# ScalarE's and VectorE's order, and the value product's place, in an attention and group-norm kernel

## The chip, the cores and the metric

One core of a Trainium2 chip runs the kernel. The time is device microseconds of one execution; the median of several executions is compared. The engines have one queue each and run their instructions in the order written: TensorE (PE in the profile, its weight loads PEld), VectorE (DVE), ScalarE (ACT), GpSimd (POOL) and SyncE (SP), which only starts transfers here. They wait for each other through semaphores.

## What is computed

```python
# x: (32, 128, 1024), y = ctx_4096: (32, 128, 1024), weights 128x128, 8 heads
q = Wq @ y + bq;  k = Wk @ y + bk;  v = Wv @ x + bv          # per batch, (heads, 16, 1024)
scores = einsum('bhdl,bhel->bhde', q, k) / sqrt(128)         # over channels: 16x16 per head
out = einsum('bhde,bhel->bhdl', softmax(scores), v)
o = Wo @ out + bo + x
result = (o - mean(o)) * rsqrt(var(o) + 1e-5) * gn_w + gn_b  # mean and variance over a whole batch item
```

## The kernel before

The scores need only y's Gram matrix G = y y^T (128x128) and y's row sums. So each of the 32 batch items becomes a short chain: Gram matrix, query product, scores, softmax, two small products that fold Wo, the softmax and Wv into one 128x128 matrix m (the identity is added for the residual), one wide product o = m x, and a normalisation whose statistics come from o's mean and variance by bn_stats. What is called a batch below is one such item.

For the Gram matrix, y comes transposed, as [128, 8 chunks, 128]. ScalarE rounds it to fp32r (`round_half`, L325), VectorE writes the rest y - rounded beside it (`rest_half`, L456), and TensorE multiplies in 8 passes, one for each chunk, with 258 columns (`gram`, L672). A pass gives rounded by rounded and rounded by rest; the second part is copied by ScalarE (`copy_cross`, L339), transposed back by TensorE (`transpose_cross`, L689) and added (`add_gram`, L475). Sums of the rest go through GpSimd (`fold_first` to `fold_last`, L243 to L284) into the same PSUM tile.

Then, for batch b: `query` (L711) and `add_query_bias` (L495); `scores` (L722) with `scale_bk` (L341); `minimum` (L506); `exponential` (L351), `invert_sum` (L517) and `normalise` (L361) make the softmax a_sb; `softmax_product` (L730) gives r in PSUM, `copy_r` (L367) copies it to r_sb, and `value_product` (L739) multiplies it by Wv. `fold_matrix` (L523) writes m_sb, the sum's waits included; `pivot_column` (L533) makes a column from which the mean is shifted. `input_product` (L746) computes o in two halves of 512 columns, each read by `statistics_of` (L542). `aggregate`, `deviation` and `square` (L548 to L566) go into `statistics` (L758), a product with ones that sums over partitions; `negative_variance`, `variance` (L568 to L600), GpSimd's power (`inverse_deviation`, L286) and ScalarE's `write_gain`, `write_shift` (L375 to L389) make scale and offset, and `output` (L391) writes the 1024 columns of the result, in one operation per batch, which SyncE stores.

All of this is software-pipelined by hand. Every engine has its own loop over t from 4 to 36 (`range(4, B + LAGS)`), and in turn t it works on up to five batches: input product and statistics of t-4, softmax and value products of t-3, query and scores of t-2, Gram matrix of t-1, rounding of t, output of t-5. The order within a turn is the order of the calls. In the last five turns (t = 32 to 36) the calls for batches that don't exist return at once, so these turns are the same order with holes. TensorE's turn is: two input halves, softmax product, query, four Gram passes, value product, four Gram passes, scores, statistics, transposition. The value product waits for r_copied. o_ps has room for two batches, so input_product(b) waits until the output of batch b-2 has been written (normed); the last batch has its two halves in g_ps and ps_ps.

## Time and profile before

| | us |
|---|---|
| median of 3 runs | 168.95 (168.01 to 169.55) |
| the profiled execution | 167.54 |
| its span, first to last instruction | 165.6 |
| mean granted clock of TensorE | 0.992 of full speed |
| median time to landing of a load of y (512 KB) | 6.1 |

The profile is of one execution, and all durations below are from it; its own time lies 1.4 us under the median. Rows of a timeline give the start, the duration, engine, line of the kernel and operation, with what is written and read; a row may stand for several instructions (x2, x4) that follow each other. Rows of a pipelined engine overlap: the next may start a tenth of a microsecond before the end of the one before, so the distance of starts, not the duration, is what an operation costs its engine. Brackets give idle time ahead of a row and what ended it. All of TensorE's products are recorded at one line, L666, and are told apart by their tiles. An fp32 product takes two weight loads and two matmuls.

### The profile page before, as it was taken

How to read it: one execution, taken by the hardware profiler on the slowest of the kernel's cores; microseconds unless marked ns; L12 is line 12 of the kernel's file. 1: busy time of each engine (PE TensorE's matmuls, PEld its weight loads, DVE VectorE, ACT ScalarE, POOL GpSimd, SP SyncE). 2: the span in 40 equal slices, each digit the busy share in tenths (PEclk: the TensorE clock that was granted, in tenths of full speed). 3: DMA queues.
4: the chain of work that ended last, by engine and by line, in shares of the span. 5: the costliest groups of instructions: out<-in, count | busy, mean ns of one | idle time of the engine just before them, and what ended most of it. 6: DMA issues, size and time to landing. Idle time of an engine off the chain costs nothing. (4 is left out here: it accounts for less than half of the span.)

```text
span 165.6 us, 3745 instructions
## 1 busy us (share of the span) xinstructions
PE 155.0 (94%) x932; PEld 121.8 (74%) x932; DVE 150.7 (91%) x686; ACT 138.9 (84%) x354; POOL 98.3 (59%) x162
## 2 busy tenths in 40 slices
PE   7998999999999999999999999999999999999720
PEld 7896888777777788877777778888777777886400
DVE  1788999999999999999999999999999999987661
ACT  3784599999999999999999989999999999977441
POOL 3049366777666676667766667666776666651110
PEclk9999999999999999999999999999999999999996
DMA  5999769999999999999999999999999987732333
GB/s 187 410 417 410 291 223 287 334 330 333 354 381 298 303 350 364 352 345 346 344 351 313 366 340 340 340 336 334 334 356 377 364 311 262 251 130 101 124 145 139
DMA packets 14276, 50.82 MB, mean 307 GB/s; under 512 B 1712, under 2 KB 1712, under 8 KB 14256
## 3 DMA queue, kind: packets, MB, share of 16 engines
q1 hardware_dynamic: 13824, 50.08, 83.4%
q10 hardware_dynamic: 432, 0.53, 0.9%
q8 instruction: 7, 0.11, 0.3%
q14 instruction: 13, 0.11, 0.2%
HBM read 33.82 MB, written 16.78 MB: 305 GB/s over the span
## 5 line engine op out<-in xcount | busy, mean ns | idle before, releaser
L666 PE MATMUL o_ps<-x_sb,m_sb 128*128 128x512 f32 x124 | 60.8, 613 | 0.0
L666 PE MATMUL g_ps<-hl_sb 128*128 128x258 f32 x256 | 46.4, 304 | 0.0
L456 DVE TENSOR_TENSOR hl_sb<-y_sb,hl_sb 128x512 fp32r<-128x512 f32 x64 | 44.0, 692 | 0.0
L325 ACT CAST hl_sb<-y_sb 128x512 fp32r<-128x512 f32 x64 | 40.0, 629 | 2.1 <-DMA y_sb<-in_ctx_dram 2.0
L546 DVE BATCH_NORM_STATS2 bn<-o_ps 128x6 f32<-128x512 f32 x62 | 40.3, 687 | 1.6 <-PE o_ps L666 1.6
L404 ACT ACTIVATE out_sb<-o_ps,shift,gain 128x1024 f32<-128x1024 f32 x31 | 37.5, 1210 | 0.1
L252 POOL TENSOR_TENSOR lsuma<-hl_sb 128x256 f32<-128x256 f32 x30 | 21.9, 731 | 25.3 <-DVE hl_sb L456 25.3
L666 PEld LDWEIGHTS g_ps<-hl_sb 128*128 128x128 f32 x256 | 35.0, 191 | 0.2 <-DVE hl_sb L456 0.2
L263 POOL TENSOR_TENSOR lsumb<-hl_sb 128x256 f32<-128x256 f32 x30 | 21.9, 729 | 18.1 <-DVE hl_sb L456 18.1
L666 PEld LDWEIGHTS o_ps<-x_sb,m_sb 128*128 128x128 f32 x124 | 21.2, 191 | 14.8 <-issue 14.8
L274 POOL TENSOR_TENSOR lsum<-lsuma,lsumb 128x256 f32<-128x256 f32 x30 | 22.4, 747 | 4.2 <-issue 0.4
L293 POOL TENSOR_TENSOR rstd<-veps,nhalf 128x1 f32<-128x1 f32 x32 | 17.6, 550 | 11.9 <-DVE veps L599 11.9
L666 PEld LDWEIGHTS rm_ps<-w_in,a_sb 128*128 128x128 f32 x64 | 12.0, 189 | 14.9 <-ACT a_sb L365 7.8
L365 ACT ACTIVATE a_sb<-a_sb,zinv 128x128 f32<-128x128 f32 x32 | 12.9, 402 | 7.5 <-DVE zinv L521 7.5
L358 ACT ACTIVATE a_sb<-sc_sb,smin 128x128 f32<-128x128 f32 x32 | 12.9, 402 | 3.4 <-DVE smin L513 3.3
L284 POOL TENSOR_TENSOR lsum<-lsum 128x128 fp32r<-128x128 f32 x30 | 14.3, 476 | 2.4
L666 PE MATMUL st_ps<-st_in,onesn 128*128 128x3 f32 (+2 forms) x66 | 10.5, 229 | 3.0 <-DVE st_in L538 1.5
L666 PE MATMUL rm_ps<-r_sb,w_in 128*128 128x128 f32 x64 | 12.6, 278 | 0.5 <-ACT r_sb L373 0.4
L666 PEld LDWEIGHTS st_ps<-st_in,onesn 128*128 128x128 f32 x66 | 9.8, 188 | 4.3 <-DVE st_in L564 3.8
L666 PE MATMUL ps_ps<-w_in,p_sb 128*128 128x128 f32 x64 | 12.5, 277 | 0.0
L666 PE MATMUL ps_ps<-wqT,g_sb 128*128 128x128 f32 x64 | 12.5, 277 | 0.0
L349 ACT ACTIVATE sbk_sb<-bkB,s_sb 128x128 f32<-128x128 f32 x32 | 12.3, 386 | 0.1
(76 smaller groups left out, 287.8 us busy)
## 6 DMA issues: line engine op xcount, KB each, us to landing
y_sb<-in_ctx_dram SPq DMA_DIRECT2D x32, 512.0 KB, 6.1
x_sb<-in_x_dram SPq DMA_DIRECT2D x32, 512.0 KB, 6.9
out_dram<-out_sb SPq DMA_DIRECT2D x31, 512.0 KB, 6.0
w_in<-in_weights_dram ACTq DMA_DIRECT2D x1, 256.0 KB, 5.6
out_dram<-out_sb ACTq DMA_DIRECT2D x1, 256.0 KB, 2.6
out_dram<-out_sb SPq DMA_DIRECT2D x1, 256.0 KB, 2.8
cols<-in_columns_dram ACTq DMA_DIRECT2D x1, 3.0 KB, 3.5
```

The costliest lines, as they stand in the source:

```text
L252: nc.gpsimd.tensor_tensor(lsuma[:, :, :], part[:, 0:HCH // 2, :], part[:, HCH // 2:HCH, :], ALU.add).then_inc(lsuma_ready, 1)
L263: nc.gpsimd.tensor_tensor(lsumb[:, :, :], part[:, 0:HCH // 2, :], part[:, HCH // 2:HCH, :], ALU.add).then_inc(lsumb_ready, 1)
L274: nc.gpsimd.tensor_tensor(lsum2[:, :, :], lsuma[:, :, :], lsumb[:, :, :], ALU.add).then_inc(lsum2_ready, 1)
L284: nc.gpsimd.tensor_tensor(lsum[:, b % 2, :], lsum2[:, 0, :], lsum2[:, 1, :], ALU.add).then_inc(lsum_ready, 1)
L293: nc.gpsimd.tensor_tensor(rstd[:, b % 2:b % 2 + 1], veps[:, b % 2:b % 2 + 1], nhalf[:, :], ALU.pow).then_inc(rstd_ready, 1)
L325: nc.scalar.copy(hl_sb[:, b % SLOTS, chunks, 0:C], y_sb[:, b % SLOTS, chunks, :]).then_inc(h_ready, 1)
L358: nc.scalar.activation(a_sb[:, b % 2, :], sc_sb[:, b % 2, :], ACT.Exp, bias=smin[:, b % 2:b % 2 + 1], scale=-1.0, accum_out=zsum[:, b % 2: ...
L365: nc.scalar.mul(a_sb[:, b % 2, :], a_sb[:, b % 2, :], zinv[:, b % 2:b % 2 + 1]).then_inc(a_ready, 1)
L404: nc.scalar.activation(out_sb[:, b % SLOTS, :], o_ps[:, b % 2, :], ACT.Identity, bias=shift[:, b % 2:b % 2 + 1], scale=gain[:, b % 2:b % 2 ...
L456: nc.vector.tensor_tensor(hl_sb[:, b % SLOTS, chunks, C:2 * C], y_sb[:, b % SLOTS, chunks, :], hl_sb[:, b % SLOTS, chunks, 0:C].bitcast(F3 ...
L546: nc.vector.bn_stats(bn[:, b % 2, half, :], o_half(b, half)).then_inc(bn_done, 1)
L666: return nc.tensor.matmul(dst, lhsT, rhs, start=start, stop=stop, **more)
```

## The change

Five things change. In ScalarE's loop, the first rounding of a batch moves to the end of the turn before, the second in between the exponential and the normalisation, and `copy_r` stands ahead of `write_shift`, so that the output follows the shift. In VectorE's loop, `invert_sum` moves behind the next turn's `copy_sum`, and `fold_matrix` and `pivot_column` go ahead of `deviation` and `square`. In TensorE's loop, the value product stands behind two Gram passes, not four. The loops end at t = 31, and each of the three engines has an order of its own written out for what the last five turns did. There, the input product of the last three batches waits for m_sb and x directly, and the variance of the last four waits for an earlier rstd. GpSimd's and SyncE's loops stay as they are.

```diff
--- before.py
+++ after.py
@@ -421,18 +421,46 @@
             scale_bk(1)
             copy_r(0)
             copy_cross(2)
-
-            for t in range(4, B + LAGS):
+            round_half(4, 0)
+
+            for t in range(4, B):
                 exponential(t - 3)
+                round_half(t, 1)
                 normalise(t - 3)
                 write_gain(t - 5)
                 scale_bk(t - 2)
+                copy_r(t - 3)
                 write_shift(t - 5)
-                copy_r(t - 3)
-                round_half(t, 0)
                 output(t - 5)
                 copy_cross(t - 1)
-                round_half(t, 1)
+                round_half(t + 1, 0)
+
+            b = LAST
+            exponential(b - 2)
+            normalise(b - 2)
+            scale_bk(b - 1)
+            write_gain(b - 4)
+            write_shift(b - 4)
+            copy_r(b - 2)
+            output(b - 4)
+            exponential(b - 1)
+            copy_cross(b)
+            normalise(b - 1)
+            scale_bk(b)
+            copy_r(b - 1)
+            write_gain(b - 3)
+            write_shift(b - 3)
+            output(b - 3)
+            exponential(b)
+            normalise(b)
+            copy_r(b)
+            write_gain(b - 2)
+            write_shift(b - 2)
+            output(b - 2)
+            write_gain(b - 1)
+            write_shift(b - 1)
+            output(b - 1)
+            output(b)
 
         @block.vector
         def _(dve):
@@ -595,6 +623,9 @@
             def variance(b):
                 if not live(b):
                     return
+                if b >= LAST - 3:
+
+                    dve.wait_ge(rstd_ready, b - 1)
                 dve.wait_ge(nvar_ready, b + 1)
                 nc.vector.tensor_scalar(veps[:, b % 2:b % 2 + 1], nvar[:, b % 2:b % 2 + 1], -1.0, EPS,
                                         ALU.mult, ALU.add).then_inc(veps_ready, 1)
@@ -638,18 +669,19 @@
             add_gram(2)
             invert_sum(1)
 
-            for t in range(4, B + LAGS):
+            for t in range(4, B):
                 copy_sum(t - 2)
                 if t > 4:
+                    invert_sum(t - 3)
                     rest_half(t - 1, 1)
                 statistics_of(t - 4, 0)
                 statistics_of(t - 4, 1)
                 add_query_bias(t - 2)
                 aggregate(t - 4)
+                fold_matrix(t - 3)
                 deviation(t - 4)
-                fold_matrix(t - 3)
+                pivot_column(t - 3)
                 square(t - 4)
-                pivot_column(t - 3)
                 rest_half(t, 0)
                 minimum(t - 2)
                 negative_variance(t - 4)
@@ -657,7 +689,60 @@
                 weighted_shift(t - 4)
                 variance(t - 4)
                 add_gram(t - 1)
-                invert_sum(t - 2)
+
+            b = LAST
+            copy_sum(b - 1)
+            invert_sum(b - 2)
+            statistics_of(b - 3, 0)
+            rest_half(b, 1)
+            add_query_bias(b - 1)
+            statistics_of(b - 3, 1)
+            aggregate(b - 3)
+            fold_matrix(b - 2)
+            minimum(b - 1)
+            deviation(b - 3)
+            pivot_column(b - 2)
+            square(b - 3)
+            invert_sum(b - 1)
+            negative_variance(b - 3)
+            variance(b - 3)
+            add_gram(b)
+            copy_sum(b)
+            weighted_shift(b - 3)
+            statistics_of(b - 2, 0)
+            add_query_bias(b)
+            fold_matrix(b - 1)
+            statistics_of(b - 2, 1)
+            minimum(b)
+            shift_by_pivot(b - 2)
+            pivot_column(b - 1)
+            invert_sum(b)
+            aggregate(b - 2)
+            statistics_of(b - 1, 0)
+            deviation(b - 2)
+            square(b - 2)
+            statistics_of(b - 1, 1)
+            negative_variance(b - 2)
+            variance(b - 2)
+            fold_matrix(b)
+            shift_by_pivot(b - 1)
+            aggregate(b - 1)
+            pivot_column(b)
+            deviation(b - 1)
+            weighted_shift(b - 2)
+            square(b - 1)
+            statistics_of(b, 0)
+            negative_variance(b - 1)
+            shift_by_pivot(b)
+            weighted_shift(b - 1)
+            variance(b - 1)
+            statistics_of(b, 1)
+            aggregate(b)
+            deviation(b)
+            square(b)
+            negative_variance(b)
+            variance(b)
+            weighted_shift(b)
             last_output()
 
         @block.tensor
@@ -669,21 +754,22 @@
                 for _ in range(count):
                     product(o_ps[:, 1, 0:P], onesn[:, :], onesn[:, :])
 
-            def gram(b, half):
-                if not live(b):
-                    return
-                pe.wait_ge(l_ready, 2 * b + 1 + half)
-                if half == 0 and b >= 1:
+            def gram(b, chunks):
+                if not live(b):
+                    return
+
+                pe.wait_ge(l_ready, 2 * b + (1 if chunks[-1] < HCH else 2))
+                if chunks[0] == 0 and b >= 1:
 
                     pe.wait_ge(g_copied, b)
                     if b <= EARLY:
                         pe.wait_ge(high_copied, b)
                     else:
                         pe.wait_ge(s_copied, b)
-                for c in range(half * HCH, (half + 1) * HCH):
+                for c in chunks:
                     mm = product(g_ps[:, 0:HL], hl_sb[:, b % SLOTS, c, 0:C], hl_sb[:, b % SLOTS, c, :],
                                  start=(c == 0), stop=(c == CH - 1))
-                if half == 1:
+                if chunks[-1] == CH - 1:
                     mm.then_inc(hl_ready, 1)
 
             def transpose_cross(b):
@@ -747,9 +833,10 @@
                 if not live(b):
                     return
                 if half == 0:
-
-                    if b == LAST:
-                        pe.wait_ge(pivot_ready, b + 1)
+                    if b >= LAST - 2:
+                        pe.wait_ge(m_copied, b + 1)
+                        pe.wait_ge(x_in[b % SLOTS], loads(b))
+
                     if 2 <= b < LAST:
 
                         pe.wait_ge(normed, b - 1)
@@ -772,38 +859,66 @@
             product(row_ps[:, :, :].rearrange("p v e -> p (v e)"), onesn[:, :],
                     diag[:, :, :].rearrange("p v e -> p (v e)")).then_inc(rows_ready, 1)
 
-            gram(0, 0)
-            gram(0, 1)
+            gram(0, range(0, HCH))
+            gram(0, range(HCH, CH))
             low_sum(0, range(0, HCH))
             transpose_cross(0)
             low_sum(0, range(HCH, CH))
             keep_busy(FILL)
             query(0)
-            gram(1, 0)
-            gram(1, 1)
+            gram(1, range(0, HCH))
+            gram(1, range(HCH, CH))
             scores(0)
             transpose_cross(1)
             low_sum(1, range(0, CH))
             query(1)
-            gram(2, 0)
+            gram(2, range(0, HCH))
             softmax_product(0)
-            gram(2, 1)
+            gram(2, range(HCH, CH))
             value_product(0)
             scores(1)
             transpose_cross(2)
             statistics(-1)
 
-            for t in range(4, B + LAGS):
+            for t in range(4, B):
                 input_product(t - 4, 0)
                 input_product(t - 4, 1)
                 softmax_product(t - 3)
                 query(t - 2)
-                gram(t - 1, 0)
+                gram(t - 1, range(0, 2))
                 value_product(t - 3)
-                gram(t - 1, 1)
+                gram(t - 1, range(2, HCH))
+                gram(t - 1, range(HCH, CH))
                 scores(t - 2)
                 statistics(t - 4)
                 transpose_cross(t - 1)
+
+            b = LAST
+            input_product(b - 3, 0)
+            query(b - 1)
+            input_product(b - 3, 1)
+            softmax_product(b - 2)
+            gram(b, range(0, HCH))
+            value_product(b - 2)
+            scores(b - 1)
+            gram(b, range(HCH, CH))
+            input_product(b - 2, 0)
+            statistics(b - 3)
+            transpose_cross(b)
+            softmax_product(b - 1)
+            input_product(b - 2, 1)
+            query(b)
+            value_product(b - 1)
+            scores(b)
+            input_product(b - 1, 0)
+            input_product(b - 1, 1)
+            softmax_product(b)
+            statistics(b - 2)
+            value_product(b)
+            input_product(b, 0)
+            statistics(b - 1)
+            input_product(b, 1)
+            statistics(b)
 
 
 # ---- launch: one core; inputs and outputs as the reference has them ----
```

## Rows read from the trace of the kernel before

**Rows 1.** The page's first part: busy time, share of the span, instructions.
```profile
PE 155.0 (94%) x932; PEld 121.8 (74%) x932; DVE 150.7 (91%) x686; ACT 138.9 (84%) x354; POOL 98.3 (59%) x162
```

**Rows 2.** Timeline of ScalarE (start us, us, engine, line, operation), full-width outputs.
```profile
22.54 1.21 ACT L404 ACTIVATE out_sb<-o_ps,shift,gain 128x1024 f32<-128x1024 f32 x1
...
141.62 1.21 ACT L404 ACTIVATE out_sb<-o_ps,shift,gain 128x1024 f32<-128x1024 f32 x1
```

**Rows 3.** Timeline of TensorE's weight loads, one turn; idle before in brackets.
```profile
85.11 0.19 PEld L666 LDWEIGHTS rm_ps<-w_in,a_sb 128*128 128x128 f32 x1 [0.24 <-ACT a_sb L365]
85.54 0.19 PEld L666 LDWEIGHTS rm_ps<-w_in,a_sb 128*128 128x128 f32 x1 [0.24 <-issue]
...
85.87 0.54 PEld L666 LDWEIGHTS g_ps<-hl_sb 128*128 128x128 f32 x4
86.35 0.31 PEld L666 LDWEIGHTS rm_ps<-r_sb,w_in 128*128 128x128 f32 x2
...
87.75 0.30 PEld L666 LDWEIGHTS st_ps<-st_in,onesn 128*128 128x128 f32 x2
88.06 0.19 PEld L666 LDWEIGHTS g_ps<-ident_r,b_sb 128*128 128x128 f32 x1
...
88.28 0.30 PEld L666 LDWEIGHTS o_ps<-x_sb,m_sb 128*128 128x128 f32 x2
```

**Rows 4.** Timeline of ScalarE, the same turn.
```profile
84.65 0.40 ACT L365 ACTIVATE a_sb<-a_sb,zinv 128x128 f32<-128x128 f32 x1 [0.23 <-DVE zinv L521]
...
85.96 0.27 ACT L373 COPY r_sb<-rm_ps 128x128 f32<-128x128 f32 x1
86.12 0.62 ACT L325 CAST hl_sb<-y_sb 128x512 fp32r<-128x512 f32 x1
86.64 1.21 ACT L404 ACTIVATE out_sb<-o_ps,shift,gain 128x1024 f32<-128x1024 f32 x1
87.74 0.26 ACT L339 CAST b_sb<-g_ps 128x128 fp32r<-128x128 f32 x1
```

**Rows 5.** Weight loads: first input product of the loop, and of two tail turns.
```profile
15.10 0.30 PEld L666 LDWEIGHTS o_ps<-x_sb,m_sb 128*128 128x128 f32 x2
...
143.26 0.30 PEld L666 LDWEIGHTS o_ps<-x_sb,m_sb 128*128 128x128 f32 x2
...
147.74 0.30 PEld L666 LDWEIGHTS o_ps<-x_sb,m_sb 128*128 128x128 f32 x2
```

**Rows 6.** Timeline of VectorE, the turn of rows 3: fold and write behind.
```profile
87.00 0.29 DVE L527 CUSTOM_DVE_ANT_0 m_sb<-rm_ps,ident 128x128 f32<-128x128 f32 x1
...
87.22 0.16 DVE L531 TENSOR_TENSOR m_sb<-rm_ps,cols 128x1 f32<-128x1 f32 x1
```

**Rows 7.** Timeline of all engines, tail turn after rows 5.
```profile
148.91 0.70 DVE L546 BATCH_NORM_STATS2 bn<-o_ps 128x6 f32<-128x512 f32 x1 [0.23 <-PE o_ps L666]
...
149.57 0.19 PEld L666 LDWEIGHTS rm_ps<-w_in,a_sb 128*128 128x128 f32 x1 [0.24 <-issue]
...
149.99 0.27 ACT L373 COPY r_sb<-rm_ps 128x128 f32<-128x128 f32 x1 [0.17 <-PE rm_ps L666]
...
150.31 0.30 PEld L666 LDWEIGHTS rm_ps<-r_sb,w_in 128*128 128x128 f32 x2 [0.32 <-ACT r_sb L373]
```

**Rows 8.** Weight loads early in the kernel: second load of a softmax product.
```profile
21.44 0.19 PEld L666 LDWEIGHTS rm_ps<-w_in,a_sb 128*128 128x128 f32 x1 [0.18 <-issue]
```

**Rows 9.** Timeline of all engines, the last turns of the tail.
```profile
155.86 0.30 PEld L666 LDWEIGHTS st_ps<-st_in,onesn 128*128 128x128 f32 x2 [0.87 <-DVE st_in L564]
...
156.29 0.29 DVE L572 TENSOR_SCALAR nvar<-st_ps 128x1 f32<-128x1 f32 x1 [0.54 <-PE st_ps L666]
...
157.82 0.39 ACT L388 ACTIVATE shift<-wshift,cols,gain 128x1 f32<-128x1 f32 x1
158.11 0.70 DVE L546 BATCH_NORM_STATS2 bn<-ps_ps 128x6 f32<-128x512 f32 x1 [0.16 <-PE ps_ps L666]
158.30 1.20 ACT L404 ACTIVATE out_sb<-o_ps,shift,gain 128x1024 f32<-128x1024 f32 x1
```

## The prediction

> **What bounds the kernel now.** The page's busy table comes first [rows 1]: TensorE 94% and VectorE 91% busy, ScalarE 84%. Two engines could be the bound; the timeline of one turn decides. The starts of the full-width output operation give the period: 22.54 to 141.62 us is 26 turns, 4.58 each [rows 2]; most are 4.57, and two are 0.17 longer for a cause that I leave as it is.
>
> In the turn at 84 to 88 us I read TensorE's weight loads, since they show when its queue moves [rows 3]. The loads of a 128-column product follow each other by 0.11 us, those of a Gram pass by 0.12 (four from 85.87 to 86.35), those of a 512-column input product by 0.43. All gaps are of these sizes but one: the two loads of the statistics at 87.75 should free the queue at 87.97, and the transposition starts at 88.06. It waits 0.09 us for ScalarE's cross copy, which starts at 87.74 and takes 0.26 [rows 4].
>
> So the turn is closed by a chain through ScalarE: second weight load of the softmax product 85.54, copy of r 85.96 (+0.42), rounding 86.12 (+0.16), output 86.64 (+0.52), cross copy 87.74 (+1.10), transposition 88.06 (+0.32), next input product 88.28 (+0.22) [rows 3, 4]. Right behind this chain stands TensorE's own sum. The first turn of the tail shows it, with no queue gap: 143.26 to 147.74 = 4.48 us [rows 5]. VectorE's fold at 87.00 comes 0.65 after the value product's first load [rows 6]; it too waits a little, but frees nothing that TensorE waits for. Shortening ScalarE's chain can return at most 4.57 - 4.48 = 0.09 us a turn, and any new wait in TensorE's queue of more than 0.09 makes the turn longer.
>
> **ScalarE's order in the loop.** The second rounding moves ahead of the normalisation, where ScalarE idled on the reciprocal; the first rounding of the next batch moves to the end of the turn; r is copied ahead of the shift. The copy of r can't come earlier: it starts 0.42 after the softmax product's second load, in the turn shown and in the tail, where the row names TensorE as what it waited for [rows 4, 7]. Behind it now stands the shift (0.16 later), and the output must wait for that: from a shift to the output with nothing between is 157.82 to 158.30 = 0.48 [rows 9]. Output after r: 0.64 instead of 0.68. The chain gets 0.04 shorter, no more; a rounding of 0.52 has been exchanged for a latency of 0.48. ScalarE's sum is the same, and it had slack. The rounding that moves forward, by about 2.8 us, reads a `y` tile whose load was issued two turns earlier (over 9 us, against a median landing of 6.1 in the page's list of DMA issues), so I cost that at nothing; were it late, ScalarE and with it the exponential would stop by the lateness.
>
> The normalisation gets later. It stood behind 0.23 idle [rows 4]; neighbouring ScalarE rows overlap by 0.09 to 0.11, so the rounding starts 0.09 before the idle time did and takes 0.52: 84.65 + 0.52 - 0.23 - 0.09 = 84.85, and a_sb is ready at about 85.25. The softmax product's first load stood at 85.11; its second, which sets the rest, at 85.54. The first may slip to 85.43. Early in the kernel a_sb held one first load back to 21.07, by 0.06; the second, at 21.44, has 0.18 idle before it instead of 0.24, and so was on its beat [rows 8]. Cost nothing, with 0.1 us of cover.
>
> **The value product behind two Gram passes.** This is the term that decides. The value product needs the r copy. From the softmax product's second load to the copy is 0.42, from the copy to the value product's load 0.32: 149.57, 149.99, 150.31 [rows 7]; the trace has this wait of 0.74 in three places, two in the tail and one ahead of the loop. It is a latency through ScalarE and can't be hurried by any of the edits. Before, four Gram passes and the query product stood between: 85.54 to 86.35 is 0.81, which covers 0.74 with 0.07 to spare. Now only 0.33 + 2 x 0.12 = 0.57 of work stands between. The queue is in order, so TensorE waits 0.74 - 0.57 = 0.17 us in every turn, and behind the waiting load stand six Gram passes, scores, statistics and transposition. The cross copy is then ready in time (chain 0.04 shorter, TensorE 0.17 later: 88.02 against 88.14), so the old wait of 0.09 is gone. Turn: 4.48 + 0.17 = **4.65 us** against 4.57.
>
> Bounds for the stall: 0.17 from the rows above; not under 0.13 if the queue wins back the 0.01 to 0.02 by which loads behind a stall follow closer (150.31, two loads, next at 150.52), and 0.06 if the first of the value product's loads, whose weights are constant (w_in), is done ahead. I take 0.17. Over the 28 turns from t = 4 to 31: the two long ones kept (+0.34), 28 x 4.65 + 0.34 = 130.54, where the stretch from the first input load at 15.10 to 143.26 [rows 5] is 128.16. **+2.4 us.**
>
> Does TensorE load constant weights while the product behind them still waits for r? The trace says no: the load itself has 0.32 us idle before it, put down to r_sb [rows 7]. The Trainium skill (TensorE: Matmul & The Clock Gate, Architectural detail: the array is 16× 32×32, not 1× 128×128) says that TensorE's queue can pull a weight load ahead of matmuls in flight. By that rule one load of 0.11 would leave the stall, and the sum would be 28 x (4.54 - 4.57) instead of 28 x (4.65 - 4.57).
>
> **VectorE's order.** Fold and pivot ahead of the deviation, reciprocal behind the copy of the sum: no work added. The fold follows the value product, which lands 0.07 earlier in the turn (0.24 of Gram passes less in front, 0.17 of stall more), and the reordering takes out the 0.1 or so by which single operations waited for the one before. VectorE got through the same work in 4.57 and has 4.65 now. Nothing gained, since TensorE waits for none of it; with the cover gone it would be at most the fold's own 0.37 [rows 6].
>
> **The last five steps.** Old: 143.26 to the span's end at 165.6, 22.4 us. New, in TensorE's order from the same point, with 0.86 for an input half and 0.22 for a pair of loads: input, query, input, softmax product (2.16), four Gram passes 0.48, stall 0.15, value product 0.45, scores 0.46, four passes 0.48, input 0.86 = 5.04; statistics of batch 28, whose variance starts 0.43 later (155.86 to 156.29): 5.47; from there to the output 2.0 (156.29 to 158.30) [rows 9], 2.1 with the r copy in the way: 7.57. The input product of batch 30 writes the same half of o_ps, so it waits for the output of 28: 7.57 + 1.26 = 8.83, a wait of nearly 0.9 in the new order. Then two input halves and the softmax product: 10.77; r and value product: 11.40; the fold's last write is done 0.65 + 0.22 + 0.15 + 0.05 = 1.07 later [rows 6]: 12.47; input half, statistics 30, and bn_stats of the second half 1.17 after its load (147.74 to 148.91) [rows 5, 7]: 14.72. Old: 158.11 - 143.26 = 14.85. What follows is unchanged, 7.5 us. **-0.1 us.** Bounds: TensorE's work in the tail sums to about 12.3, plus 0.3 and 7.5, so no order of it can end under 20.1 (-2.2); on the other side each ScalarE wait in the written order can add what it waits, some +1. The new waits on rstd for the variance are for values ready a step earlier: nothing.
>
> **Sum.** Span 165.6 + 2.4 - 0.1 = 167.9, the profiled execution 167.54 + 2.3 = 169.8. It ran 1.4 under the median of the runs (168.95), so the median becomes 168.95 + 2.3 = **171.2 us**. Its own range, with stall 0.13 to 0.17 and half a microsecond for the tail either way, is 169.5 to 171.8.
>
> **The rivals.**
> - VectorE is the true bound (faster). For it: 91% busy and a fold that starts just as the value product lands. If the stall is below 0.09 and removing VectorE's waits carries the turn to TensorE's sum of 4.48, it is 28 x -0.09 - 0.1: 166.4. It decides from a stall under 0.09. Against it: rows 7. Chance 0.12.
> - The weights are loaded ahead, stall 0.06: turn 4.54, 28 x -0.03 - 0.1: 168.0. The page named above states that rule. Chance 0.12.
> - The tail's order saves up to the 2.2 that TensorE's work allows, because outputs come earlier than I chain them: 169.0 to 170. For it: old tail turns show idle time at each product. Chance 0.15.
> - The softmax product becomes late: if ScalarE's rounding starts only after the accumulator read has ended and the normalisation after the rounding has (0.19 and 0.62 instead of 0.10 and 0.52), a_sb is 0.24 later, beyond the cover by about 0.08, and the turn is 4.73: 28 x 0.16 - 0.1: 173.3. Chance 0.13.
> - My forecast: 0.48.
>
> **How the numbers follow.** A change of under 1% (1.7 us) is about what a measurement of this kernel can't tell from none. Faster by over 1% is the first rival and a few combinations: 0.15. Within 1% (167.3 to 170.6): the second and third, and a tenth of my forecast's: 0.29. Slower: 0.56. The range from 167.9 to 173.0 leaves out the first rival and half of the fourth.
>
> **What would show it.** In the profile after: idle time on the weight loads of rm_ps<-r_sb,w_in of 0.1 us or more in every turn, put down to ScalarE's r copy (hardly any in the loop before); outputs 4.65 apart; transposition without a wait; the shift 0.16 after the r copy and the output 0.48 after the shift; in the tail a gap before the input product of batch 30. Outputs 4.5 apart or less, or no wait at the value product, would prove me wrong; so would a stretch behind batch 28's first input product shorter than 21.5 us.

## The result

| | before | after |
|---|---|---|
| median, us | 168.17 (167.8 to 169.55, 10 runs) | 169.45 (168.97 to 169.89, 10 runs) |
| ratio | | 1.0067, 95% interval 1.004 to 1.0095 |
| profiled execution, its span | 167.54, 165.6 | 169.89, 167.6 |

The change makes the kernel slower, by 0.4 to 0.95%. The direction was forecast, the size was not: 2.3 us were forecast, 1.1 to 1.3 came, and the 169.45 lies just below the forecast's own range (169.5 to 171.8), though inside the wide one (167.9 to 173.0). The two profiled executions are 2.0 us apart in span; over the runs whose spans are known (58 of before, 10 of after), the median span goes from 165.55 to 167.25 us, 1.7 us. The profile of after is of the longest of its ten executions, and that of before (167.54) lies under all ten of before.

The outputs of ScalarE in the profile after, first and 27th, as in [rows 2] (start, duration, engine, line, operation):

```profile
22.85 1.21 ACT L404 ACTIVATE out_sb<-o_ps,shift,gain 128x1024 f32<-128x1024 f32 x1
...
143.25 1.20 ACT L404 ACTIVATE out_sb<-o_ps,shift,gain 128x1024 f32<-128x1024 f32 x1
```

120.40 us for 26 turns, 4.63 each; the forecast was 4.65, before it was 4.57. Only one turn is longer than 4.64 (by 0.06), where before two were longer by 0.17. TensorE's weight loads in one turn of the loop, as in [rows 3]:

```profile
84.82 0.30 PEld L751 LDWEIGHTS o_ps<-x_sb,m_sb 128*128 128x128 f32 x2
...
86.37 0.46 PEld L751 LDWEIGHTS rm_ps<-w_in,a_sb 128*128 128x128 f32 x2 [0.39 <-ACT a_sb L365]
86.76 0.30 PEld L751 LDWEIGHTS ps_ps<-wqT,g_sb 128*128 128x128 f32 x2
86.98 0.30 PEld L751 LDWEIGHTS g_ps<-hl_sb 128*128 128x128 f32 x2
87.38 0.30 PEld L751 LDWEIGHTS rm_ps<-r_sb,w_in 128*128 128x128 f32 x2
87.60 0.30 PEld L751 LDWEIGHTS rm_ps<-cols,r_sb 128*128 128x128 f32 x2
87.82 0.79 PEld L751 LDWEIGHTS g_ps<-hl_sb 128*128 128x128 f32 x6
...
89.00 0.30 PEld L751 LDWEIGHTS st_ps<-st_in,onesn 128*128 128x128 f32 x2
89.23 0.19 PEld L751 LDWEIGHTS g_ps<-ident_r,b_sb 128*128 128x128 f32 x1
...
89.45 0.30 PEld L751 LDWEIGHTS o_ps<-x_sb,m_sb 128*128 128x128 f32 x2
```

The softmax product's second load starts at 86.64 (the row of the two ends at 86.37 + 0.46, and one load lasts 0.19), which is 1.82 after the input product's, on its old beat, although a_sb let the first one go only at 86.37. The value product follows at 87.38: 0.74 later, the latency of [rows 7], with only the query product and two Gram passes (0.57 of work, counted from the second load on) in between. The statistics at 89.00 and the transposition at 89.23 follow without a gap: the wait of 0.09 from [rows 3] is gone. ScalarE in the same turn, as in [rows 4]:

```profile
85.92 0.40 ACT L365 ACTIVATE a_sb<-a_sb,zinv 128x128 f32<-128x128 f32 x1
...
87.07 0.27 ACT L373 COPY r_sb<-rm_ps 128x128 f32<-128x128 f32 x1 [0.27 <-PE rm_ps L751]
87.23 0.39 ACT L388 ACTIVATE shift<-wshift,cols,gain 128x1 f32<-128x1 f32 x1
87.71 1.20 ACT L404 ACTIVATE out_sb<-o_ps,shift,gain 128x1024 f32<-128x1024 f32 x1
88.87 0.27 ACT L339 CAST b_sb<-g_ps 128x128 fp32r<-128x128 f32 x1
```

The copy of r at 87.07 (0.43 after the load) has idle time in front and is put down to TensorE; the shift is 0.16 behind it, and the output another 0.48. This is the turn as it was foreseen, operation by operation. In the tail (all engines, from its first input load):

```profile
144.99 0.30 PEld L751 LDWEIGHTS o_ps<-x_sb,m_sb 128*128 128x128 f32 x2
...
152.60 1.20 ACT L404 ACTIVATE out_sb<-o_ps,shift,gain 128x1024 f32<-128x1024 f32 x1
...
153.92 0.30 PEld L751 LDWEIGHTS o_ps<-x_sb,m_sb 128*128 128x128 f32 x2 [0.83 <-issue]
153.95 1.96 PE L751 MATMUL o_ps<-x_sb,m_sb 128*128 128x512 f32 x4 [0.67 <-ACT out_sb L404]
...
156.48 0.30 PEld L751 LDWEIGHTS rm_ps<-r_sb,w_in 128*128 128x128 f32 x2
...
157.51 0.16 DVE L559 TENSOR_TENSOR m_sb<-rm_ps,cols 128x1 f32<-128x1 f32 x1
...
157.72 0.30 PEld L751 LDWEIGHTS g_ps<-x_sb,m_sb 128*128 128x128 f32 x2 [0.72 <-DVE m_sb L559]
...
158.35 0.53 PEld L751 LDWEIGHTS st_ps<-st_in,onesn 128*128 128x128 f32 x2 [0.33 <-DVE st_in L592]
...
159.97 0.70 DVE L574 BATCH_NORM_STATS2 bn<-ps_ps 128x6 f32<-128x512 f32 x1
```

TensorE waits for batch 28's output (152.60 to 153.80; the matmul's row names it, the load's row has the wait as "issue") and does batch 30's input product at 153.92, 8.93 after the tail's start (8.83 was worked out). The value product follows at 11.49 (11.40), but the fold behind it writes its last column only at 157.51, 1.03 behind the value product's load, and the input product of the last batch is at 12.73 instead of 12.47. From there it is the old tail: bn_stats of the last half at 14.98 (14.72 foreseen, 14.85 before) and the end 7.6 later. The tail takes 22.61 us, 0.27 more than the 22.34 before.

### The profile page after: what moved, and what is told of

It reads as the page before. It is cut to its first block and busy times, and to the rows that moved or that the text cites. A ratio compares the mean times of both kernels' runs of the same rounds, so it can differ in the third digit from the quotient of the medians.

```text
span 167.6 us, 3752 instructions
## 1 busy us (share of the span) xinstructions
PE 157.3 (94%) x932; PEld 121.5 (73%) x932; DVE 150.6 (90%) x686; ACT 139.0 (83%) x354; POOL 97.9 (58%) x162
## 5 line engine op out<-in xcount | busy, mean ns | idle before, releaser
L751 PE MATMUL g_ps<-hl_sb 128*128 128x258 f32 x256 | 47.0, 308 | 0.0
L574 DVE BATCH_NORM_STATS2 bn<-o_ps 128x6 f32<-128x512 f32 x62 | 41.2, 692 | 1.4 <-PE o_ps L751 1.4
L325 ACT CAST hl_sb<-y_sb 128x512 fp32r<-128x512 f32 x64 | 39.0, 614 | 1.8 <-DMA y_sb<-in_ctx_dram 1.8
L751 PEld LDWEIGHTS g_ps<-hl_sb 128*128 128x128 f32 x256 | 35.5, 194 | 0.2 <-DVE hl_sb L484 0.2
L373 ACT COPY r_sb<-rm_ps 128x128 f32<-128x128 f32 x32 | 8.5, 265 | 9.1 <-PE rm_ps L751 8.8
L751 PE MATMUL rm_ps<-r_sb,w_in 128*128 128x128 f32 x64 | 15.6, 326 | 0.0
L751 PE MATMUL rm_ps<-w_in,a_sb 128*128 128x128 f32 x64 | 12.5, 277 | 0.0
```

Source lines behind the costliest of these rows:

```text
L325: nc.scalar.copy(hl_sb[:, b % SLOTS, chunks, 0:C], y_sb[:, b % SLOTS, chunks, :]).then_inc(h_ready, 1)
L574: nc.vector.bn_stats(bn[:, b % 2, half, :], o_half(b, half)).then_inc(bn_done, 1)
L751: return nc.tensor.matmul(dst, lhsT, rhs, start=start, stop=stop, **more)
```

## The experiments

From v2_only on, all were timed in five rounds beside the kernel before; ratios have 95% intervals, and are not exactly the quotients of two medians. "Turn" is the median distance of outputs in the loop, "tail" the time from the first input load of the 29th batch to the end of the span.

| kernel | turn, us | tail, us | ratio to before |
|---|---|---|---|
| before | 4.57 | 22.34 | 1 |
| after | 4.63 | 22.61 | 1.0067 (1.004 to 1.0095) |
| v2_only | 4.62 | 22.48 | 1.0098 (1.0067 to 1.013) |
| v4_after | 4.61 | 22.64 | 1.0061 (1.0039 to 1.0083) |
| loop_only | 4.63 | 22.67 | 1.0109 (1.0074 to 1.0143) |
| tail_only | 4.57 | 22.63 | 1.0003 (0.9985 to 1.002) |
| act_only | 4.55 | 22.48 | 0.9954 (0.9935 to 0.9973) |
| dve_only | 4.61 | 22.64 | 1.0079 (1.0051 to 1.0107) |
| shift_first | 4.48 | 22.34 | 0.9846 (0.9815 to 0.9878) |
| shift_first_v2 | 4.63 | 22.54 | 1.0079 (1.0053 to 1.0106) |
| v3_after | 4.61 | 22.65 | 1.0051 (1.0036 to 1.0066) |
| v3_short_pool | 4.52 | 22.59 | 0.9925 (0.9905 to 0.9945) |
| v3_dev_first | 4.52 | 22.63 | 0.9928 (0.9908 to 0.9949) |

**The value product's place alone (v2_only).**

```diff
-                gram(t - 1, 0)
+                gram(t - 1, range(0, 2))
                 value_product(t - 3)
-                gram(t - 1, 1)
+                gram(t - 1, range(2, HCH))
+                gram(t - 1, range(HCH, CH))
```

> The kernel before with one edit: the value product stands behind two Gram passes instead of four. Theory A (TensorE's queue stands at the value product until r is copied, and this stall sets the turn): outputs 4.63 us apart as in the kernel after, against 4.57; every value product's first load 0.74 us behind the softmax product's second; median +1.2 to +1.9 us against before. Rival B (the lengthening comes from ScalarE's or VectorE's new order): outputs stay 4.53 to 4.57 apart and the median within 0.3 us of before.

Turn 4.62, ratio 1.0098. Second load of the softmax product and first of the value product:

```profile
91.02 0.19 PEld L666 LDWEIGHTS rm_ps<-w_in,a_sb 128*128 128x128 f32 x1 [0.24 <-issue]
...
91.75 0.30 PEld L666 LDWEIGHTS rm_ps<-r_sb,w_in 128*128 128x128 f32 x2
```

0.73 us, as in the kernel after. This one edit is enough for the turn of the kernel after, as theory A has it. Whether the new orders of ScalarE and VectorE would be enough too, v2_only can't say; the next kernel does.

**The value product put back into the kernel after (v4_after).**

```diff
-                gram(t - 1, range(0, 2))
+                gram(t - 1, range(0, HCH))
                 value_product(t - 3)
-                gram(t - 1, range(2, HCH))
```

> The kernel after with one edit undone: the value product stands behind four Gram passes again. Theory A: no stall at the value product; the turn follows ScalarE's chain, shorter by 0.04: outputs 4.53 us apart; median 0.8 us under before (28 x -0.04, and +0.24 for the tail). Rival B (the new orders of ScalarE and VectorE cost the time): outputs 4.6 us apart or more, median at or above that of the kernel after.

Here theory A failed and rival B's turn came: 4.61 us, not 4.53. With the stall gone, something else holds the turn at nearly the same length, and the ratio is 1.0061 where the kernel after has 1.0067. The stall alone (v2_only) and the new orders alone (this kernel) each give about the whole loss; they don't add up. All engines between the fold and the statistics product, and TensorE's loads around it:

```profile
87.36 0.29 DVE L555 CUSTOM_DVE_ANT_0 m_sb<-rm_ps,ident 128x128 f32<-128x128 f32 x1
87.45 0.46 POOL L284 TENSOR_TENSOR lsum<-lsum 128x128 fp32r<-128x128 f32 x1
...
87.64 0.28 DVE L586 TENSOR_TENSOR st_in<-mv,cp 128x1 f32<-128x1 f32 x1
...
87.85 0.21 DVE L566 SCALAR_TENSOR_TENSOR st_in<-colsum,x_sb,m_sb 128x1 f32<-128x1 f32 x1
...
87.98 0.21 DVE L592 SCALAR_TENSOR_TENSOR st_in<-st_in,mv 128x1 f32<-128x1 f32 x1
...
87.86 0.30 PEld L751 LDWEIGHTS ps_ps<-sbk_sb,wqT 128*128 128x128 f32 x2
88.24 0.30 PEld L751 LDWEIGHTS st_ps<-st_in,onesn 128*128 128x128 f32 x2
```

The last pair of scores loads, at 87.86, should free TensorE's queue at about 88.09; the statistics product starts at 88.24, 0.05 after VectorE's square ends. The square stands last in a row behind the fold, and the deviation in that row takes 0.28 us and ends at 87.92, just after GpSimd's last fold (87.45 + 0.46 = 87.91). Two questions came of it: is VectorE's order alone enough, and why is the deviation slow?

**The two orders one at a time (act_only, dve_only).** act_only has ScalarE's loop order of the kernel after, dve_only VectorE's, and both go through the last turns as before.

```diff
@@ act_only, ScalarE's loop @@
+            round_half(4, 0)
...
                 exponential(t - 3)
+                round_half(t, 1)
                 normalise(t - 3)
                 write_gain(t - 5)
                 scale_bk(t - 2)
+                copy_r(t - 3)
                 write_shift(t - 5)
-                copy_r(t - 3)
-                round_half(t, 0)
                 output(t - 5)
                 copy_cross(t - 1)
-                round_half(t, 1)
+                round_half(t + 1, 0)
@@ dve_only, VectorE's loop @@
                 copy_sum(t - 2)
                 if t > 4:
+                    invert_sum(t - 3)
...
-                deviation(t - 4)
                 fold_matrix(t - 3)
-                square(t - 4)
+                deviation(t - 4)
                 pivot_column(t - 3)
+                square(t - 4)
...
-                invert_sum(t - 2)
```

> The kernel before with ScalarE's new loop order alone (and the old way through the last turns). Theory A (the turn is ScalarE's chain softmax product, r copy 0.42, shift 0.16, output 0.48, cross copy 1.10, transposition 0.32, next input 0.22): outputs 4.52 us apart, long turns of 4.7 still there, median 1.0 us under before. Rival: the later normalisation delays the softmax product's second load, turn 4.6 or more, median above before.

> The kernel before with VectorE's new loop order alone. Theory D (fold, write, deviation, pivot and square now stand in a row between the value product and the statistics product, which waits for the square; before, the deviation was done ahead of the fold): value product to next input product 2.63 - 0.65 + ... as in the kernel with four passes, outputs 4.61 us apart, 0.1 us idle in front of each statistics product, median +1.1 us. Rival: VectorE's order costs nothing, as the prediction had it: 4.57, median within 0.3 us of before.

VectorE's order costs 4.61 - 4.57 = 0.04 a turn and 0.8% by itself, the turn that theory D has: with the value product behind four passes, this part, which the prediction costed at nothing, is not free. Its deviation takes 0.27 us in the median, where before has 0.16, so theory D's reason (more operations in a row) need not be the whole one. ScalarE's order by itself is a gain of 0.5%: 0.7 us where 1.0 was expected, turn 4.55 and not 4.52. VectorE's square takes 0.26 us there in the median where before has 0.21: it starts 0.22 us into GpSimd's last fold and ends 0.01 to 0.02 behind it. Whether that is the missing 0.03 was not tried by itself.

**The last five steps (tail_only, loop_only).** tail_only takes over the written-out steps alone; loop_only runs the new loops on to t = 36 instead.

```diff
@@ tail_only, on before, on each of the three engines @@
-            for t in range(4, B + LAGS):
+            for t in range(4, B):
...
+            b = LAST
+            (the calls that the change writes out, with its waits; without invert_sum(b - 2))
@@ loop_only, on after, on each of the three engines @@
-            for t in range(4, B):
+            for t in range(4, B + LAGS):
...
-            b = LAST
-            (the calls written out, with their waits)
```

> The kernel before, with only the own order of the last five steps taken over. Theory A: turns 4.57 us as before, the stretch from the tail's first input load to the end 22.6 us against 22.4, with a wait of about 0.8 us in front of the input product of batch 30: median +0.1 to +0.4 us. Rival C: the tail is 1 us or more shorter or longer.

> The kernel after without its own order for the last five steps: the loops run on to t = 36 in the new order. Theory A (the loop carries the loss, the tail little): turns 4.63 us, tail within 0.4 us of 22.4, median within 0.4 us of the kernel after. Rival C (the written-out tail gives back or costs a microsecond): median 1 us or more away from the kernel after.

tail_only: the tail is 0.29 us longer in the profile, and the ratio can't be told from 1. loop_only lies above the kernel after by 0.4% (the intervals overlap), inside theory A's 0.4 us by the spans (167.3 against 167.25) but not by the medians (169.93 against 169.45). So the tail is no source of the loss and no gain of a microsecond either. Between the execution's time and its span lie 2.73 us in loop_only, 2.17 in the kernel after and 2.3 in the kernel before; why these differ stays open.

**A chain without the shift (shift_first), and the stall by itself (shift_first_v2).** The order is ScalarE's of the kernel after, with `write_shift` ahead of `copy_r`; VectorE's old order with the new place of the reciprocal; value product behind four passes, or two.

```diff
                 scale_bk(t - 2)
-                copy_r(t - 3)
                 write_shift(t - 5)
+                copy_r(t - 3)
                 output(t - 5)
```

> ScalarE's new loop order, but with the shift written before the copy of r; VectorE's fold order of before, with only the reciprocal behind the copy of the sum; value product behind four Gram passes; the last turns as before. Theory A: neither rounding nor the shift's latency stands between the r copy and the output, so ScalarE's chain is 4.04 us and only TensorE's own sum is left: outputs 4.48 us apart, median 2.4 us under before. Rival: the 0.06 of cover of the softmax product is not enough, turn 4.53 or more, median under 1.2 us better.

> The same as shift_first, but with the value product behind two Gram passes. Nothing else limits the turn here, so the pair measures the stall by itself. Theory A: 4.48 + 0.15 = 4.63 us a turn, median 28 x 0.15 = 4.2 us above shift_first, 1.7 above before. Rival (TensorE makes up for the stall): the pair within 1 us of each other.

shift_first is the fastest kernel here: 165.69 us against 168.03, ratio 0.9846 (five runs; the quotient of the two medians is 0.986). Its rows of ScalarE and TensorE:

```profile
84.52 1.20 ACT L404 ACTIVATE out_sb<-o_ps,shift,gain 128x1024 f32<-128x1024 f32 x1
...
85.98 0.27 ACT L339 CAST b_sb<-g_ps 128x128 fp32r<-128x128 f32 x1 [0.25 <-PE g_ps L667]
...
86.12 0.30 PEld L667 LDWEIGHTS st_ps<-st_in,onesn 128*128 128x128 f32 x2
...
86.34 0.19 PEld L667 LDWEIGHTS g_ps<-ident_r,b_sb 128*128 128x128 f32 x1
...
86.56 0.30 PEld L667 LDWEIGHTS o_ps<-x_sb,m_sb 128*128 128x128 f32 x2
...
88.54 0.37 ACT L388 ACTIVATE shift<-wshift,cols,gain 128x1 f32<-128x1 f32 x1
...
88.82 0.26 ACT L373 COPY r_sb<-rm_ps 128x128 f32<-128x128 f32 x1
89.01 1.21 ACT L404 ACTIVATE out_sb<-o_ps,shift,gain 128x1024 f32<-128x1024 f32 x1
```

The shift fits into the time in which ScalarE waits for r anyway; the output comes 0.19 after the copy, so the cross copy at 85.98 waits for TensorE and no longer the other way round, and loads follow at 86.12, 86.34, 86.56 without a gap. The turn is TensorE's sum, 4.48. It differs from act_only in two things, the shift's place and VectorE's reciprocal behind the copy of the sum. The reciprocal did not bring the normalisation forward (1.20 us behind the input product's first load, 87.76 - 86.56, against 1.19 in act_only), so the rows speak for the shift, but no run has it alone. With the value product behind two passes it becomes 4.63: the stall measured by itself is 0.15 us a turn, 3.9 us in the median. A loop 2% shorter than before becomes one 1% longer by moving one product two passes forward.

**Three passes (v3_after).**

```diff
-                gram(t - 1, range(0, 2))
+                gram(t - 1, range(0, 3))
                 value_product(t - 3)
-                gram(t - 1, range(2, HCH))
+                gram(t - 1, range(3, HCH))
```

> The kernel after with the value product behind three Gram passes, between the two (4.63 us a turn) and the four (4.61) already measured. Theory E (two limits that move against each other: TensorE's stall for r, which ends 0.74 after the softmax product's second load, and the chain value product, fold, deviation, pivot, square, statistics, 1.98 from the value product's first load to the next input product): the first load comes 2.56 us after the input product's, so 2.56 + 1.98 = 4.54 us a turn, 0.08 less than both neighbours; median 0.7 us under before for the loop, +0.1 for the tail. Rival F (the new orders cost 0.04 a turn wherever the value product stands): 4.61 to 4.63 us, median 0.6% above before.

Theory E failed too: 4.61, not 4.54. The stall at the value product was down to about 0.05 (0.74 of latency, 0.69 of work in between), but the deviation had become slower still. GpSimd, VectorE and TensorE in one turn:

```profile
87.72 0.47 POOL L284 TENSOR_TENSOR lsum<-lsum 128x128 fp32r<-128x128 f32 x1
...
87.86 0.35 DVE L586 TENSOR_TENSOR st_in<-mv,cp 128x1 f32<-128x1 f32 x1
...
88.52 0.19 PEld L751 LDWEIGHTS st_ps<-st_in,onesn 128*128 128x128 f32 x1
```

The deviation starts at 87.86 inside GpSimd's last fold (87.72 to 88.19) and ends at 88.21. Its durations in the loop, minimum, median and maximum in ns, from the views of the tile st_in: before,

```profile
L558 DVE TENSOR_TENSOR st_in<-mv,cp x24: 158/159/374, 31.9 to 137.3; 128x1 f32<-128x1 f32 x24
```

in the kernel after, with two passes,

```profile
L586 DVE TENSOR_TENSOR st_in<-mv,cp x24: 148/202/350, 32.8 to 139.2; 128x1 f32<-128x1 f32 x24
```

with four,

```profile
L586 DVE TENSOR_TENSOR st_in<-mv,cp x24: 150/270/280, 32.3 to 138.5; 128x1 f32<-128x1 f32 x24
```

and with three:

```profile
L586 DVE TENSOR_TENSOR st_in<-mv,cp x24: 149/356/365, 32.5 to 138.6; 128x1 f32<-128x1 f32 x24
```

Where no more than 0.16 us of GpSimd's sum or fold is left when the deviation starts, it takes its own 0.15 to 0.16 us; where more is left, it lasts until GpSimd is done: the nearer the two starts lie, the longer. The deviation is a VectorE operation with both inputs in SBUF.

**Which cause (v3_short_pool, v3_dev_first).** Both are v3_after with one more edit. The first shortens GpSimd's operation and leaves VectorE's order as it is (it leaves out the last addition for 120 of the 128 columns), the second takes the deviation out of its way.

```diff
-                nc.gpsimd.tensor_tensor(lsum[:, b % 2, :], lsum2[:, 0, :], lsum2[:, 1, :], ALU.add).then_inc(lsum_ready, 1)
+                n_cols = C if b < EARLY + 2 else 8
+                nc.gpsimd.tensor_tensor(lsum[:, b % 2, 0:n_cols], lsum2[:, 0, 0:n_cols], lsum2[:, 1, 0:n_cols],
+                                        ALU.add).then_inc(lsum_ready, 1)
@@ v3_dev_first, VectorE's loop @@
+                deviation(t - 4)
                 fold_matrix(t - 3)
-                deviation(t - 4)
-                pivot_column(t - 3)
                 square(t - 4)
+                pivot_column(t - 3)
```

> The kernel after with the value product behind three Gram passes, and from batch 4 on GpSimd's last fold adds only 8 of its 128 columns, so that the column sums of the other channels are stale: that part of the computation is left out, and GpSimd's operation gets shorter. Theory P (in all kernels with the fold ahead of the deviation, VectorE's deviation, 0.15 us long by itself, lies across GpSimd's last fold and ends only when that ends, 0.20 to 0.36 us): deviation back at 0.15 to 0.2, square 0.07 earlier or more, turn 4.52 us (ScalarE's chain) against 4.61, median 2.5 us under the kernel with three passes. Rival (the deviation is slow because its operand has just been written, or because of the fold in front of it): deviation stays at 0.35 and the turn at 4.61.

> The kernel after with the value product behind three Gram passes and VectorE's old order (deviation, fold, square, pivot). Theory P: the deviation is out of the way before the value product lands, and the square stands right behind the fold: no idle time in front of the statistics product, turn 4.52 us, set by TensorE's sum with a stall of 0.03 and by ScalarE's chain; median 0.8% under before with 0.1 us for the tail. Rival F (the new orders cost 0.04 in any case): 4.6 us or more.

Both give 4.52 us and 0.7% under before. In v3_short_pool the deviation is back at its own length:

```profile
L588 DVE TENSOR_TENSOR st_in<-mv,cp x24: 148/151/151, 32.0 to 136.0; 128x1 f32<-128x1 f32 x24
```

The operations in front of it on VectorE are the same as in v3_after; so GpSimd's operation is the cause of the long deviation, and not VectorE's fold in front. And since v3_short_pool, with the new order, has the same turn as v3_dev_first with the old one, it is this collision and not the row of operations in itself that costs the 0.09 us. The Trainium skill (SBUF — State Buffer, SBUF: two separate sides) says that a VectorE instruction with two SBUF inputs and a GpSimd instruction that reads SBUF exclude each other, whichever starts second being blocked to the end of the first; for VectorE starting second behind GpSimd's sums and folds these traces agree, down to an operation of one column a partition (0.15 us alone, 0.36 behind a fold of 0.47). The trace shows the block as a longer duration, not as idle time. They don't agree for every operation of GpSimd. In the kernel before, VectorE's rest, with both inputs in SBUF, starts in each turn inside GpSimd's power of one column, and lasts as long as where GpSimd is idle:

```profile
84.44 0.55 POOL L293 TENSOR_TENSOR rstd<-veps,nhalf 128x1 f32<-128x1 f32 x1
...
84.58 0.68 DVE L456 TENSOR_TENSOR hl_sb<-y_sb,hl_sb 128x512 fp32r<-128x512 f32 x1
```

That is 0.68 to 0.69 us in all 24 such turns, and the same in the 24 rests beside an idle GpSimd; what sets the power apart from the folds was not tested.

The same thing explains one of the two long turns of the kernel before. One turn there has GpSimd's sum late, and it reaches into the deviation:

```profile
95.63 0.73 POOL L274 TENSOR_TENSOR lsum<-lsuma,lsumb 128x256 f32<-128x256 f32 x1 [0.43 <-issue]
...
96.00 0.37 DVE L558 TENSOR_TENSOR st_in<-mv,cp 128x1 f32<-128x1 f32 x1
...
96.57 0.33 DVE L564 SCALAR_TENSOR_TENSOR st_in<-st_in,mv 128x1 f32<-128x1 f32 x1
...
97.15 0.30 PEld L666 LDWEIGHTS st_ps<-st_in,onesn 128*128 128x128 f32 x2 [0.21 <-DVE st_in L564]
```

GpSimd sat idle for 0.43 us with nothing to wait for; its sum (until 96.36) covers the deviation (until 96.37, 0.37 instead of 0.16), and the statistics load waits 0.21. The square behind it is longer too (0.33 instead of 0.21, under the fold that follows the sum). In the same kernel ScalarE pauses once without a reason in the profile. What makes an engine pause was not tested.

## Why the prediction was right and wrong

- **Right: what sets the turn of the kernel after.** The stall at the value product, its mechanism and its place were the prediction's, and v2_only and the pair with shift_first show it. The weights of the value product are constant (w_in) and were not loaded ahead of its wait: 4.62 and 4.63 us, not 4.54. So the use that the prediction's second rival makes of the Trainium skill (TensorE: Matmul & The Clock Gate, Architectural detail: the array is 16× 32×32, not 1× 128×128) did not come true. What it states there is that loads are pulled ahead of matmuls in flight; here a wait stands in front of the load, and no run tests the rule itself.
- **Right: ScalarE's order.** The chain became 0.04 shorter, the second weight load kept its beat although the first was late, and the rounding's tile was there. In act_only, where nothing stalls, the gain is 0.5%.
- **Wrong: "28 x 4.65 + 0.34".** This is the step that failed: the mechanism came, and the loop's term was put at +2.4 us and measured +1.4. The stall makes the turn 0.15 longer and not 0.17 (halfway between the bounds of 0.13 and 0.17), which is 28 x 0.02 = 0.6 us; and the two long turns were kept in the sum, but the kernel after has only one, by 0.06: 0.3 us. The loop took 129.59 us instead of 130.54, where 128.16 is the time before. The stall alone doesn't take the long turns in: v2_only has it, and still has turns of 4.81 and 4.75. In the kernel after GpSimd pauses as it does before, but the deviation, in its new place, is not under the late sum:

```profile
96.78 0.73 POOL L274 TENSOR_TENSOR lsum<-lsuma,lsumb 128x256 f32<-128x256 f32 x1 [0.43 <-issue]
...
97.57 0.15 DVE L586 TENSOR_TENSOR st_in<-mv,cp 128x1 f32<-128x1 f32 x1
```

ScalarE's pause does not show in that execution, and why stays open.
- **Wrong by a little: the last five steps.** -0.1 was worked out and +0.27 measured. The chain through batch 28's output was 0.1 off; the last fold's column came 1.03 behind the value product's load instead of the 0.87 of the turn in rows 3 and 6. In the time it makes no measurable difference.
- **Wrong, but hidden: VectorE's order at no cost.** In the kernel after it costs nothing, since the stall covers it; that the error doesn't show in the forecast time is luck, for the turn that this order gives without the stall (4.61, v4_after) lies only 0.02 below. By itself it costs 0.8%. The prediction costed the order from TensorE's waits in the trace of before and allowed "at most the fold's own 0.37" without cover; it didn't ask what VectorE's operations would then overlap, and the deviation moved into GpSimd's last fold. With three passes that collision is the whole cost (v3_short_pool); with four no run separates it from the longer row of operations behind the fold.
- **The base.** The forecast was put on the median of three runs, 168.95; 10 and 19 runs gave 168.17 and 168.07. 0.8 us of the distance between 171.2 and 169.45 is this, the largest single part. The sum on the profiled execution, 169.8, is close to the 169.89 of the profiled execution after, but by luck: the one lies under all ten runs of before, the other is the highest of after.

In spans: forecast +2.3, less 0.6 and 0.3 in the loop, plus 0.4 in the tail, is 1.8; 1.7 is measured between the medians. The two profiled executions are 2.0 apart, because the first input load also comes 0.3 later in the one of after (15.40 against 15.10; it lies between 14.82 and 15.40 in the kernels here). In times, the median of after is 1.3 above that of the ten runs of before and 1.4 above that of the 58 (168.0); of the 0.3 to 0.4 that is missing there, 0.15 lies outside the span (2.3 in the median before, 2.2 after), and the rest is unexplained.

## What to carry to other kernels

Before a consumer is moved forward in an in-order queue, measure producer to copy to consumer as one latency (here 0.74 us, PSUM through ScalarE back to TensorE) and count the work that is left between: what is missing is lost in every turn, whatever it does for the engines behind. When two limits lie within 0.1 us of each other, removing one shows the other, so cost each edit alone and in the pair. And a tiny operation that the output waits for belongs in idle time ahead of the critical copy, not behind it: from act_only to shift_first the shift moves ahead of the copy (and the reciprocal behind another one, which the rows show to matter little), and the ratio goes from 0.9954 to 0.9846. Last, when an order is changed by hand, look at what the moved operation will overlap on other engines, and not only at who waits for it.

## What the runs showed of the hardware

A one-column operation of VectorE with two SBUF inputs took 0.15 us alone and in the loop up to 0.36 when it started within GpSimd's fold of 128 columns (0.47 us), ending within 0.03 of the fold's end in every turn of the loop in which it was longer; with a fold of 8 columns (0.20 us) it was back at 0.15. GpSimd's power of one column (0.55 us) had no such effect on VectorE's rest of 512 columns (0.68 us with and without it). In these kernels a weight load of TensorE behind a wait did not start early, even where its own weights are constant: the product's wait held it for as long as 0.32 us [rows 7].
